# Expert gate and up weights made the stationary operand and fetched tile by tile, with 12 shared chunks in the expert loop, two of them behind it

## The reference, cut to what matters

```python
def _L0_ffn_ref(x, router_w, router_bias, gate_w, up_w, down_w, sgate_w, sup_w, sdown_w):
    TOPK = 4                                            # of 32 experts, D = H = 128
    flat = x.reshape(B * T, D)                          # 8192 tokens
    scores = softmax(flat @ router_w.T + router_bias)
    topk_scores, topk_idx = jax.lax.top_k(scores, TOPK)
    topk_scores = topk_scores / topk_scores.sum(axis=-1, keepdims=True)
    h = silu(einsum('nd,ehd->neh', flat, gate_w)) * einsum('nd,ehd->neh', flat, up_w)
    expert_out = einsum('neh,edh->ned', h, down_w)
    out = (sel(expert_out, topk_idx) * topk_scores[:, :, None]).sum(axis=1)
    return out + silu(flat @ sgate_w.T) * (flat @ sup_w.T) @ sdown_w.T   # shared expert, 512 wide
```

## Time and profile before

| | |
|---|---|
| median of three runs | 1078.01 us |
| the profiled execution's own time | 1076.78 us |
| its span | 1074.9 us |
| stage 3, first `gate_up` to the end of the last `down` | 594.2 to 994.3 us |
| last scatter of stage 3 starts | 996.9 us |
| first load of `y_rows` issued | 999.1 us |
| tail from there to the end of the span | 75.8 us |
| busy over the span: PE, DVE, ACT, POOL | 89%, 68%, 57%, 62% |

### The profile page before, as it was taken

How to read it: one execution, slowest core, us unless ns; L and a number is a source line. 1 busy time by engine, 2 the same in 40 slices (tenths; PEclk the granted TensorE clock), 3 DMA queues, 4 the chain that set the end, 5 groups by cost and what they waited for, 6 DMA issues and landing times.

```text
span 1074.9 us, 26031 instructions
## 1 busy us (share of the span) xinstructions
PE 954.3 (89%) x6592; PEld 728.6 (68%) x6593; DVE 733.7 (68%) x2496; ACT 613.1 (57%) x2213; POOL 669.9 (62%) x935
## 2 busy tenths in 40 slices
PE   4988888988888888889769999999999999999987
PEld 2777777777777777777655666666667666776544
DVE  3788888888888988888755344444444444454696
ACT  3667766767677777767532455555555555555211
POOL 1267777777777777777662477677777677777100
PEclk9999999999999999999879899999999999999999
DMA  5511111111111111111315433333333333331794
GB/s 154 200 37 33 36 37 37 33 33 39 36 36 33 39 38 33 39 38 62 110 33 98 99 96 95 95 91 90 94 93 96 93 92 93 93 94 32 273 363 146
DMA packets 91623, 90.43 MB, mean 84 GB/s; under 512 B 21277, under 2 KB 73098, under 8 KB 91204
## 3 DMA queue, kind: packets, MB, share of 16 engines
q1 hardware_dynamic: 71876, 55.07, 18.4%
q0 software_dynamic: 17408, 33.87, 9.6%
q10 hardware_dynamic: 2304, 1.07, 0.6%
HBM read 49.72 MB, written 42.31 MB: 86 GB/s over the span
## 4 chain that ended last, share of the span: by engine, by line
PE 43%; DVE 17%; issue 16%; DMA 12%; POOL 9%; ACT 1%; POOLq 1%; SPq 0%; DVEq 0%; ACTq 0%
DMA x_rows<-payload,slot 11%; PE ps L1071 11%; POOL x_rows L432 9%; PE ps L1082 9%; DVE payload L751 3%; PE ps L1108 3%; PE ps L1066 3%; PE ps L1076 3%; PE ps L1092 3%; PE ps L1098 3%; PE ps L1035 2%; DVE kvbd L677 2%; PE ps L942 2%; DVE w_gu L881 1%; PE ps L1044 1%
## 5 line engine op out<-in xcount | busy, mean ns | idle before, releaser
L443 POOL DMA_INDIRECT y_rows<-y_sb,xin x288 | 283.0, 983 | 141.8 <-issue 80.5
L432 POOL DMA_INDIRECT x_rows<-payload,slot x256 | 251.2, 981 | 132.7 <-DVE slot L762 70.4
L836 DVE TENSOR_TENSOR h<-sg,ps 128x128 f32<-128x128 f32 x288 | 82.6, 287 | 181.6 <-ACT sg L575 181.6
L1071 PE MATMUL ps<-w_gu,xT 128*128 x576 | 175.9, 388 | 8.2 <-issue 8.2
L1082 PEld LDWEIGHTS ps<-w_dn,hT 128*128 128x128 f32 x576 | 94.4, 190 | 105.8 <-ACT hT L580 73.0
L942 PE MATMUL ps<-vt,pT 128*128 128x108 f32 x1024 | 145.6, 287 | 0.0
L580 ACT COPY hT<-ps 128x128 f32<-128x128 f32 x288 | 76.4, 265 | 109.7 <-PE ps L1076 107.4
L942 PEld LDWEIGHTS ps<-vt,pT 128*128 128x128 f32 x1024 | 130.7, 200 | 11.3 <-issue 10.9
L1082 PE MATMUL ps<-w_dn,hT 128*128 x576 | 129.9, 308 | 8.1 <-DVE y_sb L842 6.2
L575 ACT ACTIVATE sg<-ps 128x128 f32<-128x128 f32 x288 | 80.5, 280 | 72.7 <-PE ps L1071 48.8
L842 DVE TENSOR_SCALAR y_sb<-ps,xin 128x128 f32<-128x128 f32 x288 | 99.7, 346 | 24.2 <-PE ps L1082 22.5
(11 more groups left out here) (136 smaller groups left out, 1978.4 us busy)
## 6 DMA issues: line engine op xcount, KB each, us to landing
xin<-x_rows SPq DMA_DIRECT2D x288, 65.0 KB, 1.9
w_gu<-y_rows SPq DMA_DIRECT2D x16, 1024.0 KB, 8.6
y_rows<-y_sb,xin POOLq DMA_INDIRECT x288, 2.3
w_gu<-in_gu SPq DMA_DIRECT2D x2, 2048.0 KB, 10.3
x_rows<-payload,slot POOLq DMA_INDIRECT x256, 2.4
out<-x_all SPq DMA_DIRECT2D x16, 256.0 KB, 5.8
w_dn<-in_dn SPq DMA_DIRECT2D x1, 2048.0 KB, 8.8
ctx_sb<-in_ctxT SPq DMA_DIRECT2D x64, 29.2 KB
```

What stands on the lines that cost most here:

```text
L432: nc.gpsimd.indirect_dma_start(x_rows, bass.IndirectOffsetOnAxis(ap=slot[:, v, k:k + 1], axis=0), payload[:, v, k, :], None).then_inc(sent ...
L443: nc.gpsimd.indirect_dma_start(y_rows, bass.IndirectOffsetOnAxis(ap=xin[:, u, D:D + 1].bitcast(U32), axis=0), y_sb[:, u, :], None, bounds_ ...
L836: nc.vector.tensor_tensor(h[:, u % 2, :], sg[:, u % 2, :], ps_gu[u % 2][:, H:2 * H], ALU.mult).then_inc(h_d[u % PER], 1)
L1071: after(nc.tensor.matmul(ps_gu[u % 2][:, 0:2 * H], xT[:, u % 2, :], w_gu[:, bass.ds(e * (2 * H), 2 * H)], start=True, stop=True), xT_d, n, ...
```

## The change

`gate_up` now takes the expert's weights as the stationary operand and `xT` as the moving one: two matmuls of 128 columns, for gate and for up. The result is transposed, so `hidden` writes `hT` directly; `turn_h`, `h_turned` and the buffer `h` are gone, and their bank serves as a second one for `turn_x`. The weights are no longer resident: SP fetches 128 KB for each tile into one of 18 buffers `w_t`, ahead of the tile's rows, on the same semaphore. The order inside a slot is now `down(u-2)`, `gate_up(u)`, `turn_x(u+2)` on PE and `result(u-2)`, `hidden(u)` on DVE. A body may hold a whole chunk, with units at slots 1, 5, 9 and 13. Body 0 holds none, bodies 1 to 12 hold one each, bodies 13 to 15 none; two chunks are left for the tail.

```diff
-MID = 8
+MID = 12
-UNIT_AT = (6, 14)
+UNIT_AT = (1, 5, 9, 13)
-        ps_xT, ps_gu, ps_hT, ps_dn, ps_g, ps_u, ps_y = bank[0], bank[1:3], bank[3], bank[4], bank[5], bank[6], bank[7]
+        ps_xT, ps_gu, ps_dn, ps_g, ps_u, ps_y = (bank[0], bank[3]), bank[1:3], bank[4], bank[5], bank[6], bank[7]
         def bodies(body, fori):
-            body(0, 0, 0, first=True)
-            body(1, 0, 1)
-            with fori(1, MID - 1) as c:
-                body(2 * c, c, 0)
-                body(2 * c + 1, c, 1)
-            body(TG - 2, MID - 1, 0)
-            body(TG - 1, MID - 1, 1, last=True)
+            body(0, first=True)
+            with fori(1, MID + 1) as j:
+                body(j, mixed=True)
+            with fori(MID + 1, TG - 1) as j:
+                body(j)
+            body(TG - 1, last=True)
             def load_tiles(j):
                 firsts = numbers(sp, tab_sb, j * TW, U3, XROWS - 128)
+                es = numbers(sp, tab_sb, j * TW + EAT, U3 + 2, E - 1)
                 for u in range(U3):
                     need(sp, y_sent[u], 16 * j)
+                    sp.dma_start(w_t[:, u, :], gu[:, bass.ds(es[u + 2] * (2 * H), 2 * H)]).then_inc(xin_in[u], 16)
                     sp.dma_start(xin[:, u, :], x_rows[bass.ds(firsts[u], 128), :]).then_inc(xin_in[u], 16)
...
                 for u in range(U3):
-                    hidden(n, u)
                     if not (first and u < 2):
                         result(n, u - 2)
-                    if u - 2 in UNIT_AT:
-                        mixed_hidden(c, 2 * half + UNIT_AT.index(u - 2))
-                if half:
-                    mixed_take(c)
+                    hidden(n, u)
+                    if mixed and u - 2 in UNIT_AT:
+                        mixed_hidden(j, UNIT_AT.index(u - 2))
+                if mixed:
+                    mixed_take(j)
...
-            def gate_up(n, u, e):
-                after(nc.tensor.matmul(ps_gu[u % 2][:, 0:2 * H], xT[:, u % 2, :], w_gu[:, bass.ds(e * (2 * H), 2 * H)],
-                                       start=True, stop=True), xT_d, n, u).then_inc(gu_p[u % PER], 1)
-            def turn_h(n, u):
-                after(nc.tensor.transpose(ps_hT[:, 0:128], h[:, u % 2, :], ident),
-                      h_d, n, u).then_inc(hT_p[u % PER], 1)
+            def gate_up(n, u):
+                after(nc.tensor.matmul(ps_gu[u % 2][:, 0:H], w_t[:, u % U3, 0:H], xT[:, u % 2, :],
+                                       start=True, stop=True), xT_d, n, u)
+                nc.tensor.matmul(ps_gu[u % 2][:, H:2 * H], w_t[:, u % U3, H:2 * H], xT[:, u % 2, :],
+                                 start=True, stop=True).then_inc(gu_p[u % PER], 1)
```

More of the change, by code:

```diff
@@ L170, in build @@
         sg = sb("sg", [128, 2, H])
-        h = sb("h", [128, 2, H])
         hT = sb("hT", [128, 2, 128])
@@ L245, in counts @@
         def counts(eng, j, last=0, dma=False):
-            per_body, each = (1, 16) if dma else (U3 // PER, 1)
+            per_body, each = (1, 32) if dma else (U3 // PER, 1)
             return [None] * dma + [each * (per_body * j + k) if isinstance(j, int) else eng.to_reg(each * (per_body * j + k))
@@ L586, in mixed_silu, with body @@
                 nc.scalar.activation(ssg[:, k % 2, :], ps_g[:, :], ACT.Silu).then_inc(ssg_d, 1)
-            def body(j, c, half, first=False, last=False):
+            def body(j, first=False, last=False, mixed=False):
                 n = counts(act, j, U3 // PER + 1)
@@ L591, in body @@
                     silu(n, u)
-                    if not (first and u == 0):
-                        h_turned(n, u - 1)
                     if not (last and u >= U3 - 2):
                         evac(n, u + 2)
-                    if u in UNIT_AT:
-                        mixed_silu(c, 2 * half + UNIT_AT.index(u))
+                    if mixed and u in UNIT_AT:
+                        mixed_silu(j, UNIT_AT.index(u))
             for u in range(2):
@@ L845, in mixed_hidden @@
             def mixed_hidden(j, k):
-                unit = 4 * (EARLY + j) + k
+                unit = 4 * (EARLY + j - 1) + k
                 need(dve, ssg_d, unit + 1)
@@ L1116, in body @@
                 for u in range(U3):
[L1117 to L1120, removed]
-                        mixed_up(c, 2 * half + UNIT_AT.index(u - 1))
                     if not (first and u < 2):
                         down(n, u - 2, es[u])
-                    if not (first and u == 0):
-                        turn_h(n, u - 1)
+                    gate_up(n, u)
+                    if mixed and u in UNIT_AT:
+                        mixed_gate(j, UNIT_AT.index(u))
+                    if mixed and u - 1 in UNIT_AT:
+                        mixed_up(j, UNIT_AT.index(u - 1))
                     if not (last and u >= U3 - 2):
                         turn_x(n16, n, u + 2)
-                    if u - 3 in UNIT_AT:
-                        mixed_down(c, 2 * half + UNIT_AT.index(u - 3))
+                    if mixed and u - 3 in UNIT_AT:
+                        mixed_down(j, UNIT_AT.index(u - 3))
                     if u == EHALF - 3:
@@ L1134, in body @@
                     down(n, U3 - 2, es[U3])
-                    turn_h(n, U3 - 1)
                     down(n, U3 - 1, es[U3 + 1])
```

39 lines of the change are left out of this document (17 added, 22 removed).

## The result

The change makes the kernel slower. The median of four runs is 1111.54 us (1104.31 to 1112.03), against 1077.70 us for the kernel before in its four; the ratio is 1.0298 [1.0248, 1.0347]. The forecast was 1096 us, slower; the sign is right, the size 15.5 us too low. The profiled execution took 1111.64 us, its span is 1109.8 us at a mean granted clock of 0.949 of 2.4 GHz.

What follows compares the result with a forecast made beforehand. PE was taken to bound the loop, POOL its last three bodies, DMA the tail. Start +2.1, loop and POOL +30.6, tail -13.8 on a 1074.9 us span gave 1093.8, forecast as 1096 us; range 1085 to 1108, stretched to 1068 and 1112.

Steps and rivals of the forecast that it cites:

- stage 1's end to the first `gate_up`: Before the loop: more number reads and a weight fetch ahead of the first rows make PE start 2.1 us late.
- body 0: First loop body, no shared part: 18 slots of 1.02 us, 1.0 between bodies, 2 for low clock, 21.4 us.
- bodies 1 to 12: Loop bodies with a whole chunk of shared work: twelve at 28.2 us, 338.4 us, bound by PE.
- body 13 to the end of the last scatter: Last three loop bodies: POOL limits, 56 tiles at 1.31 us make 73.4, plus 1 us for the first result.
- Pass rate and weight loads: PE in the loop: a 128-column pass costs 0.11 us with its weight load hidden, 0.76 us of own work a slot.
- rival 4: `gate_up` in the loop: four weight loads of 0.11 us show each time, 7.7 us a body; 1164 us, chance 0.03.
- Slots without a shared part stay at 1.02: Loop slots: `down` waits for the previous tile's `result` through one bank, a circle of 1.01 to 1.02 us.
- The wait for `hs`, 0.47 us a unit: Before `mixed_down` in slot k+3: PE waits 0.36 us for `mixed_hidden`, then pays 0.11 for an unhidden load.
- The shared unit, 6.3 us: Four loop slots: 1.61 each for gate and up, and 3.21 - 0.11 for the last two, 6.3 us.
- "SP and DMA in the loop: they fit, and I cost them at nothing.": Loop weight fetches: SP needs 21.8 us a body against POOL's 23.6 and PE's 28.2, so no cost was added.
- POOL alone at the end, 56 x 1.31: Bodies 13 to 15: POOL has 56 scatters left at 1.31 us, 73.4 us, while PE finishes some 15 us earlier.
- The tail, 62 us: Behind the loop: DMA bounds, 20.7 MB at 365 to 376 GB/s plus start and end, 62 us against 75.8.

Runs made afterwards that it cites:

- e5: Changed kernel with the second bank given to `down` instead of `turn_x`: 1101.25 us, 1.0215 of the kernel before.
- e3: Changed kernel with one line moved, `mixed_hidden` ahead of the slot's `hidden` in DVE's order: 1084.65 us, 1.0064 of the kernel before.
- e6: Changed kernel with the edits of e3 and e5 together: 1071.59 us, 0.9952 of the kernel before.
- e7: Changed kernel with e3's edit and the 12 chunks spread, three units in each of 16 bodies: 1065.19 us, 0.9893 of the kernel before.
- e8: Changed kernel with e7's edits and e5's two banks for `down`: 1047.06 us, 0.9736 of the kernel before.
- e4: Changed kernel without weight fetches and their number loads, slot u always using expert u's weights: 1098.46 us, 1.0187 of the kernel before.

## Why the prediction was right, and where it was short

By its own steps, on the changed kernel's trace. The forecast's span was 1093.8, the measured one 1109.8: 16.0 too low. 6.0 of that is stage 1's chance. The other 10.0 repeat in every run (9.7 to 10.1), and are the prediction's. The measured median lies above the forecast's own range of 1085 to 1108 us, and only just under the 1112 to which it was stretched.

| term | forecast | measured | off by |
|---|---|---|---|
| stage 1's end to the first `gate_up` | 24.2 | 24.0 | -0.2 |
| body 0 | 21.4 | 24.7 | +3.3 |
| bodies 1 to 12 | 338.4 | 347.3 | +8.9 |
| body 13 to the end of the last scatter | 74.4 | 74.4 | 0.0 |
| last scatter's end to the first load | 1.3 | 1.2 | -0.1 |
| tail | 62.0 | 60.2 | -1.8 |

- *Pass rate and weight loads.* Right. The halves of `gate_up` and `turn_x` start 0.22 us apart (739.90, 740.12, 740.35), 0.11 for each pass. The four weight loads of `gate_up` are hidden; rival 4 does not hold for the loads of this kernel. Nor does the rule of the Trainium skill ("TensorE: Matmul & The Clock Gate", on packing small matmuls) that stands behind it.
- *Slots without a shared part stay at 1.02.* Right for this kernel: 1.01 in the unit, and 1.02 between 1031.08 and 1032.10 in its last body, where the circle `down`, `result`, `down` is alone. e5 confirms that the bank is what holds it.
- *The wait for `hs`, 0.47 us a unit.* Right, with its place and its cause: 0.42 between passes in the trace, and e3 takes it away by moving one line. It is most of the loss: without it the kernel stands at 1084.65 us, 0.6% over the kernel before and not 3.0%.
- *The shared unit, 6.3 us.* Right in mechanism, short in size: 6.49. The two slots of gate and up are 1.64 and not 1.61 (a pass is 0.11, where I had rounded to 0.108), and the last two slots are 3.21, not 3.10, mostly because `mixed_hidden` follows on `hidden` after 0.29 and not 0.21 us. Four units make 0.19 x 4 = 0.76 of that in a body; slots 0 and 17 with the step between bodies took 0.2 less than the 3.04 given them. The net is 28.8 for a body against 28.2: 7.2 of the 8.9 us.
- *"SP and DMA in the loop: they fit, and I cost them at nothing."* This step failed for body 0 and body 1. I held SP's 21.8 us against POOL's 23.6 and the mixed bodies' 28.2, which are the paces of the loop's middle, and not against PE in body 0, 18 x 1.02 = 18.4 us, where no unit slows it. SP's body is also 23.0 us and not 21.8; 1.2 of it is one issue that stayed 1.57 us. The wait, and the low clock behind it, show as +3.3 us in body 0 and +1.7 in body 1 (30.5 against 28.8); that a wait would also cost clock, no part of the forecast had. `turn_x` waiting for `xin` was one of the signs of being wrong that the prediction named, and it came, for these two bodies. Without fetches body 0 is 4.7 shorter, below even my 21.4, since the 2 us that I had given to the first slots were too much. In the later mixed bodies the step was right: the same 28.8 us with and without fetches, at a DMA share of 0.59 (I had allowed 0.72).
- *POOL alone at the end, 56 x 1.31.* Right in sum: 73.38 us from body 13's start to the last scatter's, and 73.3 to 73.4 in e3 to e6, whatever was done to PE. (It is 57 scatters 1.29 apart; I had 56 at 1.31, and the two errors cancel by luck.) Because it lies behind the last shared unit, no gain of PE shortens it. e7 and e8 show that it was a matter of where the units stand.
- *The tail, 62 us.* Right in what bounds it, 1.8 too long: I had 365 to 376 GB/s for the loads, and it ran at 394 in the middle.

The timeline of DVE in that tail, two steps of `combine`, shows the releaser:

```profile
1087.68 1.23 DVE L872 TENSOR_TENSOR moe<-moe 128x1024 f32<-128x1024 f32 x1 [0.61 <-DMA moe<-y_rows]
...
1091.05 1.23 DVE L872 TENSOR_TENSOR moe<-moe 128x1024 f32<-128x1024 f32 x1 [0.69 <-DMA moe<-y_rows]
```

One `combine` comes each 3.4 us, of which 2.6 to 2.7 are DVE's own, and the rest is the wait for the loads.

## What to carry to other kernels

Filler work pays where a slower engine lets the filled one wait, so spread it at the pace of the engine that sets the end. Here PE had a unit too many in each of 12 bodies to keep POOL fed, and too little to do in the rest, and the same work spread out was 19 to 27 us faster. When an order is shortened, look at what stands in front of the first instruction that another engine waits for: one line of DVE's order was worth 27 us, more than the new form of the matmuls. And hold a queue against the fastest stretch of the engine that it feeds, count what it does between two rounds, and look at the granted clock behind a wait of TensorE.

## What the runs showed of the hardware

The end of stage 1, whose code is nearly the same in all these kernels, moved between 570.5 and 578.1 us. That is up to 0.7% of the whole, and more than the 0.5% taken as the limit of what can be told; differences of that size are better read from marks behind that stage. A second bank that takes a wait away from one instruction can come back almost whole as a wait of the next (0.19 us gained and 0.18 lost in each unit of e5). In the changed kernel TensorE sat idle for 2 us up to 623.1 us, and its granted clock was 0.50 from 624 to 630 us. In e4, without that wait, the clock was 1.00 through the same body, which was 1.6 us shorter.
